# First projections in four PSUM banks, halved row maxima, spread norms and one full sweep less in a fused conv-attention, attention and recurrence kernel

## What is computed

```python
# 1. convolutional attention, 32 inner channels, softmax over all 1024 positions
q, k, v = wq @ xf, wk @ xf, wv @ xf                  # per batch, xf is (64, 1024)
out = x + wo @ (softmax(k.T @ q, axis=2) applied to v)
# 2. causal attention over tokens, 8 heads of 64
t = t + attention(layernorm(t), Wq, Wk, Wv) @ Wo
# 3. a recurrence over the 1024 positions
z = batchnorm(layernorm(t) @ W.T) * gamma + beta
y[0] = sigmoid(z[0]);  y[n] = sigmoid(z[n] + V @ y[n-1])
out = t + y
```

## Time and profile before

| | |
|---|---|
| median of 3 executions | 599.87 us (599.86 to 600.62) |
| the profiled execution's time | 600.17 us |
| its span | 598.0 us |
| TensorE, weight loads, VectorE, ScalarE, GpSimd busy | 507.9, 330.6, 406.0, 434.1, 413.2 us |
| mean granted TensorE clock | 0.958 of full speed |

### The profile page before, as it was taken

One profiled execution on the slowest core, in us unless ns is written; L12 is line 12 of the kernel. 1 busy time (PEld: TensorE's weight loads), 2 busy tenths in 40 slices (PEclk: granted clock), 3 DMA queues, 4 the chain that ended last, 5 costly groups with the idle time before them and its releaser, 6 DMA issues.

```text
span 598.0 us, 16614 instructions
## 1 busy us (share of the span) xinstructions
PE 507.9 (85%) x6778; PEld 330.6 (55%) x6778; DVE 406.0 (68%) x930; ACT 434.1 (73%) x835; POOL 413.2 (69%) x401
## 2 busy tenths in 40 slices
PE   2578967988899799989999998899999989885794
PEld 0134746655566476665766666566676566652241
DVE  3658776777886567777667687866767866207477
ACT  2147857877588588878888887687888858881873
POOL 2524765777689678888789797796879869890003
PEclk9979988999999899999999999899999979997798
DMA  9100000000000000000000000000000000000001
GB/s 233 49 1 1 3 1 19 1 4 1 2 3 2 19 2 3 3 2 20 3 2 2 3 2 19 3 2 2 2 2 2 3 1 3 3 1 2 0 1 70
DMA packets 3419, 7.44 MB, mean 12 GB/s; under 512 B 1136, under 2 KB 1424, under 8 KB 3216
## 3 DMA queue, kind: packets, MB, share of 16 engines
q1 hardware_dynamic: 2976, 5.34, 3.3%
q10 hardware_dynamic: 368, 1.05, 0.6%
HBM read 4.22 MB, written 1.05 MB: 9 GB/s over the span
## 4 chain that ended last, share of the span: by engine, by line
PE 53%; DVE 28%; POOL 7%; ACT 5%; issue 4%; DMA 1%; SPq 0%; DVEq 0%; POOLq 0%; ACTq 0%
DVE attn_partial_max L806 10%; PE bank L490 9%; PE bank L448 7%; PE bank L519 7%; POOL probs_low L1113 5%; PE bank L523 4%; DVE conv_partial_max L800 4%; PE bank L668 3%; ACT probs_high L695 3%; PE bank L411 3%; PE bank L527 3%; PE bank L525 3%; PE bank L412 3%; PE bank L475 3%; PE bank L434 2%
## 5 line engine op out<-in xcount | busy, mean ns | idle before, releaser
L1113 POOL TENSOR_TENSOR probs_low<-probs,probs_high 128x512 f16<-128x512 f32 x288 | 327.1, 1157 | 110.4 <-ACT probs_high L695 109.9
L691 ACT ACTIVATE probs<-bank 128x512 f32<-128x512 f32 x352 | 215.4, 614 | 86.1 <-PE bank L490 69.7
L806 DVE TENSOR_REDUCE attn_partial_max<-bank 128x1 f32<-128x512 f32 (+2 forms) x288 | 185.2, 685 | 93.6 <-PE bank L448 93.0
L695 ACT ACTIVATE probs_high<-bank 128x512 f16<-128x512 f32 x288 | 177.2, 615 | 0.0
L523 PEld LDWEIGHTS bank<-values_high,probs_high 128*128 128x128 f16 x1152 | 106.9, 99 | 64.3 <-issue 41.1
L523 PE MATMUL bank<-values_high,probs_high 128*128 128x65 f16 x1152 | 130.6, 197 | 7.0 <-DVE scaled_outputs L881 4.7
L525 PE MATMUL bank<-values_low,probs_high 128*128 128x64 f16 x1152 | 129.4, 195 | 0.0
L527 PE MATMUL bank<-values_high,probs_low 128*128 128x65 f16 x1152 | 128.9, 195 | 0.0
L525 PEld LDWEIGHTS bank<-values_low,probs_high 128*128 128x128 f16 x1152 | 107.9, 100 | 4.5 <-issue 0.7
L527 PEld LDWEIGHTS bank<-values_high,probs_low 128*128 128x128 f16 x1152 | 108.1, 99 | 0.0
L519 PE MATMUL bank<-values,probs 128*128 128x65 f32 x512 | 73.6, 283 | 0.0
(11 more groups left out here) (165 smaller groups left out, 726.0 us busy)
## 6 DMA issues: line engine op xcount, KB each, us to landing
x_channels<-in_x_cm SPq DMA_DIRECT2D x7, 256.0 KB, 8.0
tokens<-in_x_tm SPq DMA_DIRECT2D x1, 1024.0 KB, 11.2
out<-ln_channels SPq DMA_DIRECT2D x4, 256.0 KB, 2.0
queries_high<-minus_max_rows SPq DMA_DIRECT2D x35, 2.0 KB
attn_weights<-in_attn_w ACTq DMA_DIRECT2D x1, 512.0 KB, 7.7
attn_keys_split<-attn_keys_high SPq DMA_DIRECT2D x4, 128.0 KB, 2.2
attn_keys_split<-attn_keys_low SPq DMA_DIRECT2D x4, 128.0 KB, 2.3
x_channels<-in_x_cm ACTq DMA_DIRECT2D x1, 256.0 KB, 3.6
```

The source lines that it names most:

```text
L691: ins = nc.scalar.activation(e32[:, i % E_RING, :], o[:], ACT.Exp, scale=scale)
L695: ins = nc.scalar.activation(p_hi[:, i % P_RING, :], o[:], ACT.Exp, scale=scale)
L806: nc.vector.reduce_max(dst, o[:].rearrange("p (n w) -> p n w", n=n), AX).then_inc(s_prep_used, 1)
L1113: nc.gpsimd.tensor_tensor(out=p_lo[:, i % P_RING, :], in0=e32[:, i % E_RING, :], in1=p_hi[:, i % P_RING, :], op=ALU.subtract).then_inc(s_r ...
```

## The change

- **Start.** Batch 0's x is loaded and split in two column halves; VectorE has a constant column `one` instead of waiting for the constants. The four projections of batch 0 leave the auxiliary list and go into four banks (ST and one OT) in the order queries first half, keys first, keys second, queries second; slots begin at -12 instead of -19. GpSimd makes the identities and masks.
- **Maxima.** All four stage 1 batches use one pattern: sixteen maxima in slots first-12 to first+3, one a slot, closed and transposed by halves, projections at first-19, -17, -15, -10. The weight products move to slots 8, 10, 24, 26.
- **Norms.** `LN1_GROUPS` becomes batch 0; batch 1; batches 2 and 3. Batch 1's tiles take one slot each from 66, those of the third group one every two slots from 96, with the root steps at 75, 77, 79 and 129, 131, 133. Batch 1 is applied at slot 81 and its keys are made at 90 and 94. `scaled` is a ring of four. `pool_ln1` works without `xd`.
- **Last batch.** Its first half is normed by VectorE in slots 346 to 351, transposed in slot 350 and multiplied in 352. The second half follows the last slot with an add on VectorE, one norm instruction per tile, and transposes, copies and products by 256 columns.
- **Token transposes** leave slots 266 and 270 and come after the last products; two of the four stay in PSUM until the output is added.
- **Sweeps.** VectorE's inputs wait for ScalarE's first sigmoids only for the last chunk; `FULL_SWEEPS` is 5.

The diff, cut to its core:

```diff
-ST_RING, MX_RING, P_RING, E_RING, Q_RING = 3, 2, 10, 10, 3
+ST_RING, MX_RING, P_RING, E_RING, Q_RING, S_RING = 3, 2, 10, 10, 3, 4
...
-FULL_SWEEPS = 6
+FULL_SWEEPS = 5
...
-CONV_PREP = list(range(-20, -4))
-CONV_PREP_0 = list(range(-12, 4))
-CONV_PREP_1 = [-12 + k // 2 for k in range(16)]
+CONV_PREP = list(range(-12, 4))
...
-PROJECT_SLOTS = (-27, -25, -23, -21)
-PROJECT_SLOTS_0 = (-19, -17, -15, -13)
-PROJECT_SLOTS_1 = (-26, -24, -22, -18)
-CONV_MAXT_SLOT, CONV_MAXT_SLOTS_0, CONV_VALUES_SLOT, CONV_VALUES_SLOT_0 = -3, (-4, 4), -2, 1
+PROJECTIONS = ((False, 0), (True, 0), (True, 1), (False, 1))
+PROJECT_SLOTS = (-19, -17, -15, -10)
+CONV_MAXT_SLOTS, CONV_VALUES_SLOT, CONV_VALUES_SLOT_0 = (-4, 4), -2, 2
...
-FIRST_SLOT = -19
-LN1_GROUPS = ((0, 1), (1, B))
-LN1_SLOT = (22, 71)
-LN1_STEPS = 5
-LN1_PACE = (1, 4)
-LN1_APPLY_SLOT = (27, 92, 148, 220)
-KEY_SLOTS = ((35, 37), (100, 104), (154, 158), (226, 230))
-MATRIX_SLOTS = (0, 2, 16, 18)
+FIRST_SLOT = -12
+LN1_GROUPS = ((0, 1), (1, 2), (2, B))
+LN1_SLOT, LN1_PACE = (22, 66, 96), (0, 1, 2)
+LN1_STEP_SLOTS = ((24, 25, 26), (75, 77, 79), (129, 131, 133))
+LN1_APPLY_SLOT = (27, 81, 148, 220)
+KEY_SLOTS = ((32, 34), (90, 94), (154, 158), (226, 230))
+MATRIX_SLOTS = (8, 10, 24, 26)
...
-LN3_TRANSPOSE_SLOTS, WX_SLOTS, TOKEN_SLOTS = (248, 256), (252, 262), (266, 270)
+LN3_TRANSPOSE_SLOTS, WX_SLOTS = (248, 256, 350), (252, 262, 352)
+LAST_STATS_SLOT = 346
...
         def _(pe):
+            pe.wait_ge(s_cws, 1)
+            for k in range(4):
+                if k % 2 == 0:
+                    pe.wait_ge(s_x16, k // 2 + 1)
+                pe_project(FIRST_BANKS[k], k).then_inc(s_first, 1)
             pe_aux(0)
...
             elif what == "ln3_transpose":
                 nc.tensor.wait_ge(s_l3, k + 1)
+                if k == 2:
+                    nc.tensor.wait_ge(s_l3t, 1)
...
+            for t in range(TPC):
+                pe.wait_ge(s_l3, 4 + t)
+                ins = pe_transpose(LN_BANKS[t // 2], xh3, 3, t)
+                if t % 2:
+                    ins.then_inc(s_tr, 1)
+            pe.wait_ge(s_aux_used, len(AUXES))
+            for h in range(2):
+                pe.wait_ge(s_trc, h + 1)
+                nc.tensor.matmul(WX_BANKS[h][:, 0:HW], ffn_w[:, 0, :], xh3T[:, 3 * CW + h * HW:3 * CW + (h + 1) * HW],
                                  start=True, stop=True).then_inc(s_wxp, 1)
+            for k in (3, 2):
+                pe_transposes(T2_BANKS[k], tok, k).then_inc(s_t2, 1)
             pe.wait_ge(s_bn1, 1)
...
+            if g == LAST_STATS_SLOT:
+                nc.vector.wait_ge(s_added, half_of(UNITS - 1, 0, 1) + 1)
+                last_stats(0)
+            if 0 < g - LAST_STATS_SLOT <= 4:
+                ln3_rstd(g - LAST_STATS_SLOT - 1, B - 1, B, 0, TPC)
+            if g == LAST_STATS_SLOT + 5:
+                x, y, mean, scale = ln3_views_of_half(0, B - 1, B)
+                link(nc.vector.tensor_tensor(out=y, in0=x, in1=mean, op=ALU.subtract))
+                nc.vector.tensor_tensor(out=y, in0=y, in1=scale, op=ALU.mult).then_inc(s_l3, 1)
...
-            last_batch(0)
-            last_batch(1)
+            dve.wait_ge(s_added, HALVES - 1)
+            dve.wait_ge(s_scaled, HALVES)
+            dst = tok3[:, TPC:NT, (B - 1) * C:B * C]
+            link(nc.vector.tensor_tensor(out=dst, in0=scaled[:, (HALVES - 1) % S_RING, :, :], in1=dst, op=ALU.add))
+            last_stats(1)
+            for step in range(4):
+                ln3_rstd(step, B - 1, B, TPC, NT)
+            for t in range(TPC, NT):
+                n = t * B + B - 1
+                nc.vector.tensor_scalar(xh3[:, n * C:(n + 1) * C], tok[:, n * C:(n + 1) * C], mv[:, n, 0:1],
+                                        rstd[:, n:n + 1], ALU.subtract, ALU.mult).then_inc(s_l3, 1)
...
-                    dve.wait_ge(s_y, k + 1)
+                    if k == 3 and dst is wx16:
+                        dve.wait_ge(s_y, 4)
```

More of the change, by code:

```diff
@@ L943, in dve_norms @@
         def dve_norms(g):
-            for group in range(len(LN1_GROUPS)):
-                step, off = divmod(g - LN1_SLOT[group], LN1_PACE[group])
-                if off == 0 and 0 <= step < LN1_STEPS:
-                    dve_ln1(group, step)
+            for group, (b0, b1) in enumerate(LN1_GROUPS):
+                tiles = [(b, t) for b in range(b0, b1) for t in range(NT)]
+                if g == LN1_SLOT[group]:
+                    nc.vector.wait_ge(s_added, b1 * NC)
+                now = [tile for n, tile in enumerate(tiles) if g == LN1_SLOT[group] + n * LN1_PACE[group]]
+                if now:
+                    dve_ln1_tiles(now)
+                if g in LN1_STEP_SLOTS[group]:
+                    dve_ln1(group, LN1_STEP_SLOTS[group].index(g))
             for b in range(B - 1):
@@ L964, in last_batch @@
             link(ins)
-            for step in range(4):
-                ln3_rstd(step, B - 1, B, c * TPC, (c + 1) * TPC)
-            x, y, mean, scale = ln3_views_of_half(c, B - 1, B)
-            link(nc.vector.tensor_tensor(out=y, in0=x, in1=mean, op=ALU.subtract))
-            nc.vector.tensor_tensor(out=y, in0=y, in1=scale, op=ALU.mult).then_inc(s_l3, 1)
         @block.vector
         def _(dve):
+            link(nc.vector.memset(one[:], 0.0))
+            nc.vector.memset(one[0:1, :], 1.0).then_inc(s_one, 1)
             dve.wait_ge(s_cw, 16)
@@ L990, in _ @@
             ins.then_inc(s_init, 1)
+            for k in range(3):
+                dve_first(k)
             for g in range(FIRST_SLOT, LAST_SLOT):
@@ L1122, in pool_add @@
             dst = tok3[:, c * TPC:(c + 1) * TPC, b * C:(b + 1) * C]
-            nc.gpsimd.tensor_tensor(out=dst, in0=scaled[:, half % 2, :, :], in1=dst, op=ALU.add).then_inc(s_added, 1)
+            nc.gpsimd.tensor_tensor(out=dst, in0=scaled[:, half % S_RING, :, :], in1=dst, op=ALU.add).then_inc(s_added, 1)
         POOL_STEPS = [0]
```

315 lines of the change are left out of this document (164 added, 151 removed).

## The result

The change made the kernel **slower by 0.64%**: a median of 604.38 us (five executions, 600.72 to 606.97) against 600.1 (five, 599.86 to 600.62), ratio 1.0064, interval 1.004 to 1.0087. The forecast was 583.3, range 575 to 591. The traced execution is the fastest of the five: 600.72, span 598.9, 0.9 above the span of before. Ratios leave disturbed executions out, so they can differ from the quotient of two medians. There are two questions: where 16 forecast microseconds went in the trace, and why the ordinary execution is 3 to 6 us above it.

What follows compares the result with a forecast made beforehand. No single engine was taken as the bound: latency chains at start, end and TensorE's pauses, TensorE itself in late attention. Terms -12.4 - 1.5 + 0 - 1.7 - 3.4 + 6.6 - 0.7 - 3.4 = -16.5 gave 583.3 us, range 575 to 591.

Steps and rivals of the forecast that it cites:

- Start, -12.4: Up to item 0: x in halves and four projection banks bring item 0 to about 22.5; bounds -8 and -14.
- Convolution slots, -1.5: Slots 0 to 64: single maxima and no key stall gain, double slots and added projections cost; -1.5, bounds -7 and +5.
- the key stall: Convolution slots: the wait for batch 0's split keys and the low-clock stretch after it go, -4.5.
- Norms, 0: Spread norms: earlier keys and spread statistics gain, extra root operations and moved key work cost; 0, bounds -6 and +5.
- Token transposes, -1.7: Two token transposes leave slots 266 and 270, in a unit 2.5 us over the pitch: -1.7.
- The end, +6.6: Last batch's first half: VectorE steps stretched under GpSimd's low parts delay slot 350 and the last scale, +6.6.
- The new tail, -3.4: After the last scale: only the second half remains, averages' product 8.9 after instead of 12.4; -3.4, -4.2 at high clock.
- Sweeps: At the end: first half-sweep waits only for its last chunk, -0.7; one full sweep less, -3.4.
- Rival 1: Last batch's first half: GpSimd does not stretch VectorE there, it costs 1.4; 578 us in all, chance 0.26.
- rival 3: Sweeps: five do not suffice, the flag triggers 1024 sequential steps, 600 us more, 1190 or later; chance 0.02.
- rival 2: Start gain partly lost: low clock in the fill, slots 43 to 51 and 129 to 133 at upper bounds; 590, chance 0.25.

Runs made afterwards that it cites:

- group 1: Changed kernel with the norms of batches 1 to 3 in one group again, nothing else edited: 599.17 us, ratio 0.9975 to the kernel before.
- group 3: Changed kernel with stage 1 in the former order, last half transposed after the last slot, norms of batches 1 to 3 in one group: 591.74 us, ratio 0.9869.

## Why the prediction was wrong

**Start, -12.4: right in its number.** Item 0 came at 23.15 (22.5 forecast), and the projections in turn show that the four banks are worth 5 to 6 by themselves. But not all of the 11.7 was saved. In the kernel before, three projections of batch 1 stood in slots -10, -8 and -6; the change moves them behind slot -4. In the former order, with two of them back ahead of slot -4 and a weight product in slot 0, item 0 comes at 30.45. So up to 7.3 us of the gain are work that was moved behind item 0 and is paid for there. In the slower executions some 1 us more is gone at item 0.

**Convolution slots, -1.5 with an upper bound of +5: the step that failed.** It measured +9.2, and +12 in the slower executions. The table by items shows which term it was. Slots 0 to 16 gave their -4, and the key stall went too (items 36 to 40 take 5.6 in place of 9.0). The forecast priced what arrives in the slots after 28 at +1.5 for two more projections, in slots 33 and 38, and at "about 1.1 each" for four and a half double slots. Items 28 to 36 cost +7.7, and items 44 to 60 cost +7.7 in place of +5. Slots 28 to 35 held three auxiliary steps before and hold seven now. In the fill TensorE, ScalarE, VectorE and the one auxiliary bank go in turn: about 2.36 us for a slot with a step in slots 30 to 34, against 1.34 a slot where four of eight have one (10.72 for slots 4 to 12). The projections moved early and the pairs moved late show the cost moving with the work (72.4 against 72.5; 27.9 against 27.6). It is not all conserved: undoing the whole order costs 10 in slots -4 to 12 and gives back 6 and 7.6 in slots 28 to 60, so that with the same steps slot 60 comes 1.6 to 5.4 us sooner.

**Norms, 0 with bounds -6 and +5: wrong in one part and in its sum.** The key stall is gone (29.84 to 23.85), and the ten root operations cost 4.5 in their unit, about the 4 forecast. But the 3 us that spreading should have taken off the statistics do not show: the first two units take 56.0, where they took 51.5 before. With the norms in one group they take 57.3 in one trace (group 1) and 53.7 in another (group 3). In the changed kernel batch 1's own root step, from slot 75 on, lies ahead of a unit's closing maxima, as the one at 129 does. That the last row maxima queue behind such a step, and the low clock after it, were missing in the forecast. Its own terms also add up to between -3 and 0, and it took 0. All of slots 60 to 150 cost +4.1 to +6.9. Of this the grouping is 0.8 in the two traces that differ by it; with the norms in one group the stage still takes 131.8 against 128.3 before, and no run here tells what the other 3.5 are.

**Token transposes, -1.7:** their unit fell by 1.2, the stretch by 2.3. **The end, +6.6:** measured +7.7; taken away alone it gives 6.0 in the median. The mechanism was the forecast one, and the run without low parts there shows it. Four operations were hit, as counted. Of the Trainium skill (SBUF — State Buffer, "Who interferes with whom") the forecast used that a VectorE instruction with two SBUF inputs is fully blocked while GpSimd reads SBUF. The trace agrees for the two of that kind that were hit, L926 and L927 (1.07 and 1.08, and 0.17 without low parts). L963 and L923, with one input, took 1.17 and 1.08 as well. The 1.01 of the earlier trace rows that the forecast set beside the rule is a one-input instruction too; the two-input ones after it took 1.03 and 1.08. **The new tail, -3.4:** -2.8. **Sweeps:** -3.5 for -4.1. The full sweeps gave their 3.4 (20.90 to 17.45), and five suffice; the half sweeps took 12.7 in place of 11.3, at a mean granted clock of 0.73 in place of 0.78. Rival 1 is ruled out, rival 3 did not happen.

The chances named a slower kernel only by a failing recurrence. The way it came, several moved pieces at once at or above their upper bounds, stood in rival 2, priced at 590. At its two stages' bounds of before (+5 and +5) it would have been 595; the changed kernel's fastest execution took 600.7. Above that, the two medians of 604.38 and 605.93 hold 3.7 and 5.2 us that the forecast had no term for.

## What to carry to other kernels

Where engines take turns through one bank, as in the fill here, moving a step to slots that look free mostly moves its price. Read a slot's room from the pitch of slots that hold such a step, and do not book as a gain what was only moved behind the mark that you look at. Before a latency-bound step on VectorE is put into the steady slots, look at what queues behind it, there and on TensorE: the same transposes cost 6 us as a wait inside the loop and were no longer waited for when placed behind it. Where executions of one program spread, trace several: the fastest one alone, 0.6 us over the median of before, hid most of the 4.3 us of the medians.

## What the runs showed of the hardware

VectorE instructions with one SBUF input were stretched under GpSimd's low parts like those with two: L963 (one strided SBUF input of 4 elements) took 1.17 and L923 (one, int32) 1.08, against 0.17 and 0.17 with GpSimd idle. At the end one VectorE operation got through per low part (started 1.10 to 1.20 apart, under five low parts in 5.60). The granted clock differed between executions of one program (0.69 to 1.00 in 12 to 45). In two programs that are the same up to the sweeps, 0.53 and 1.00 in that stretch, with TensorE busy for 23 of its 33 us, made a difference of 0.2 us from slot -4 to 12. With 32 more matmuls in the fill the clock was at 0.50 in 124 to 128, between slots 52 and 60, where no trace of the unedited kernel is below 1.00.
